# One edge pass for the first normalised layer: source-tile sums taken in the message pass, scatters all ahead of it

## The chip, the cores and the metric

The kernel runs on one core of a Trainium2 chip. The metric is the device time of one launch, in microseconds (us), lower is better. Engines: PE (TensorE), DVE (VectorE), ACT (ScalarE), POOL (GpSimd), SP (SyncE, which here only starts DMAs). PEld is PE's weight load, and a "q" behind an engine's name (SPq, DVEq) is its sequencer.

## What is computed

A graph of 3125 nodes and 53125 edges (sorted by destination) passes through four residual blocks, each followed by a layer norm. The lines that matter here are those of the second and the third:

```python
# block 1: messages over the edges
m_in = concatenate([h_node[src], h_node[dst], h_edge], axis=-1)
m = silu(m_in @ msg_W1 + msg_b1) @ msg_W2 + msg_b2
agg = segment_sum(m, dst)
h_new = silu(concatenate([h_node, agg]) @ upd_W1 + upd_b1) @ upd_W2 + upd_b2
# block 2: three layers with batch statistics over all edges
for l in range(3):
    x = concatenate([h[src], e], axis=1) @ W1[l].T + b1[l]
    x = (x - mean(x, axis=0)) * rsqrt(var(x, axis=0) + 1e-5) * gamma[l] + beta[l]
    m = relu(x) @ W2[l].T + b2[l]
    h = segment_sum(m, dst)
    if l < 2: h = relu(h); e = relu(e)
```

Block 0 is a GIN network and block 3 two SAGE layers; both work on a dense adjacency count and are not touched.

## The kernel before

Edges are cut into 104 groups of 512 (`NG`, `GE`; four chunks of 128 each, `GC`), and a loop over groups is written as 13 trips (`TRIPS`) of 8 (`UNROLL`). A pass over the edges works like this, for one group: POOL gathers the source rows with four indirect DMAs (L508); SP starts the load of the edge features (L522); PE multiplies these with the weights into PSUM (L1009 in block 1, L1050 in block 2; each f32 matmul of the code is two instructions of the trace); DVE adds the gathered rows (L1631, L1810) and in block 2 takes the maximum with a row (L1815); PE scatters the 512 messages into a window of 64 nodes by one-hot matrices that DVE makes (L532, L585); ACT copies the window out (L592), PE turns it (L599) and DVE adds it to the accumulator (L607). Each engine runs its own program in order and they meet only at semaphores; rings of eight edge slots and eight gather slots decouple them.

In the profiled execution the program has these stages, by its own times: to 549 us the setup and block 0, with the edges counted; 549 to 1095 the message pass of block 1; 1095 to 1141 its update; 1141 to 1690 pass A of layer 0; 1690 to 1878 pass B of layer 0; then for each of the layers 1 and 2 a table of 68 to 70 us and a merged loop of some 500 us, to 3016; to 3280 the SAGE layers.

**The edge rows by source tile.** For the statistics of layers 1 and 2 the kernel needs, for each of 25 tiles of 128 source nodes, the sum of relu(e) over the edges that leave each node, and the Gram matrix of relu(e). So POOL first copies all edge rows (128 features and the source's number, 132 floats) into `by_tile`, in the order of their source tile: 416 indirect scatters (L2285), in 208 pairs that SP loads. 376 of them stand ahead of block 1's gathers, 40 behind them. In pass A the rows are read back as units of 512 (L2497 loads a unit's first row into a register of SP, L2498 starts the DMA), 130 units, 10 per trip. Per unit ACT applies relu and a mask (L2153, four activations), DVE makes the one-hot (L1695), PE does eight instructions of 256 columns (L1061: one-hot and features side by side), and DVE adds the two halves of the result to the source sums `tA`, at a place that it loads into a register (L1700), and to `gram` (L1706, L1707).

**The two passes of layer 0.** Layers 1 and 2 have their statistics before the loop (from the sums) and run one merged pass. Layer 0 has not: pass A computes the pre-activations, adds them (L1768), writes them to `pre_dram` (96 DMAs of 512 KB from ACT's queue), squares them on ACT and sums the squares on DVE (L1758); then come the statistics, and pass B reads the pre-activations back, applies the maximum, and scatters. Its one-hots are made by POOL (L2388) and ACT.

**Block 1's targets.** Each group needs the 64 rows of its window of destination nodes. SP loads the window's start into a register (L2479) and starts two loads of these rows, one for each half of the partitions (L2481, `tabd`); ACT and DVE split them into three bf16 parts in the loop (L2091: three casts, L1618: two subtractions), and PE takes these with a one-hot of the destinations (L1013, L1016).

## Time and profile before

| | us |
|---|---|
| median of 3 runs | 3280.3 |
| lowest and highest | 3274.34, 3285.24 |
| the profiled execution's own time | 3281.03 |
| its span in the trace | 3279.8 |
| busy in the span: PE, DVE, POOL, ACT | 2644.0 (81%), 1990.8 (61%), 2157.4 (66%), 1272.0 (39%) |
| mean DMA rate | 174 GB/s |

The profiled execution lies 0.7 us above the median, so its spans can be used as they are. The share of a busy engine over the whole span says little here, since each stage has a limit of its own. The view of stretches gives, for each stage, the busy time of each engine and the clock that was granted to PE as a share of full speed; the timelines of one engine show the pace of one group; the rows of a source line show how often and for how long an instruction ran, and what ended the idle time before it.

### The profile page before, as it was taken

The numbers are of one execution on the slowest core, as the hardware profiler recorded it, in microseconds if no ns is written. First come the engines' busy times: TensorE is split into PE (matmuls) and PEld (weight loads), VectorE is DVE, ScalarE is ACT, GpSimd is POOL, SyncE is SP. The second block draws the span as 40 slices with busy tenths as digits, with TensorE's granted clock in tenths as the row PEclk, the third lists the DMA queues.
The fourth block names the chain that finished last, engine by engine and source line by source line (L and its number), as shares of the span: only waits on it lengthen the run. The fifth ranks groups of instructions, "written<-read, shape, count | busy, mean of one in ns | idle before, by whom it ended". The sixth has DMA issues, their size and how long they took to land. (4 is left out here: it accounts for less than half of the span.)

```text
span 3279.8 us, 59515 instructions
## 1 busy us (share of the span) xinstructions
PE 2644.0 (81%) x14026; PEld 1768.6 (54%) x14026; DVE 1990.8 (61%) x3581; ACT 1272.0 (39%) x3069; POOL 2157.4 (66%) x2211
## 2 busy tenths in 40 slices
PE   5689895776776878888889998777679867777998
PEld 2234443665665567777766656555446545555444
DVE  7998596544444567777779846555554655555111
ACT  4777514433333456666667622111112211112111
POOL 2777776777777677777758657777755777775000
PEclk7799998667667798999989999999989999988999
DMA  3344556655565489999959745555534555555000
GB/s 121 105 107 108 178 155 176 192 166 164 166 167 151 133 289 320 325 324 321 322 159 328 267 142 168 154 159 155 154 107 148 169 155 155 158 157 170 42 1 20
DMA packets 305074, 570.43 MB, mean 174 GB/s; under 512 B 54466, under 2 KB 140407, under 8 KB 303511
## 3 DMA queue, kind: packets, MB, share of 16 engines
q1 hardware_dynamic: 204582, 299.39, 29.8%
q0 software_dynamic: 86528, 219.09, 22.7%
q10 hardware_dynamic: 13824, 50.34, 3.8%
q8 instruction: 58, 0.95, 0.1%
q14 instruction: 82, 0.66, 0.1%
HBM read 465.21 MB, written 103.66 MB: 173 GB/s over the span
## 5 line engine op out<-in xcount | busy, mean ns | idle before, releaser
L508 POOL DMA_INDIRECT region<-tab,region x624 | 602.3, 965 | 285.4 <-issue 203.5
L1050 PE MATMUL psum<-w_all,region 128*128 128x256 f32 x2496 | 636.7, 400 | 0.7 <-ACT region L2161 0.7
L2285 POOL DMA_INDIRECT by_tile<-stage,place x416 | 407.1, 979 | 181.0 <-issue 126.3
L1050 PEld LDWEIGHTS psum<-w_all,region 128*128 128x128 f32 x2496 | 485.0, 201 | 66.1 <-issue 2.1
L592 ACT COPY region<-psum 128x256 f32<-128x256 f32 (+1 forms) x420 | 143.3, 341 | 850.5 <-PE psum L585 850.5
L585 PE MATMUL psum<-region 128*64 128x256 f32 (+1 forms) x1664 | 223.6, 393 | 192.2 <-DVE region L1815 122.1
L508 POOL DMA_INDIRECT tN<-tab,region x312 | 302.5, 970 | 95.1 <-issue 94.8
L508 POOL DMA_INDIRECT tA<-tab,region x312 | 298.3, 956 | 95.0 <-issue 94.4
L1061 PE MATMUL psum<-region 128*128 128x256 f32 x1040 | 281.0, 418 | 82.3 <-DVE region L1695 81.7
L599 PEld LDWEIGHTS psum<-fold,region 128*128 128x128 f32 x1470 | 215.9, 207 | 154.0 <-issue 153.8
L1061 PEld LDWEIGHTS psum<-region 128*128 128x128 f32 x1040 | 208.6, 208 | 136.6 <-issue 106.0
L599 PE MATMUL psum<-fold,region 128*128 128x64 f32 x1470 | 277.1, 309 | 0.0
L585 PEld LDWEIGHTS psum<-region 128*64 128x64 f32 x1664 | 115.1, 150 | 266.2 <-issue 178.3
L508 POOL DMA_INDIRECT region<-tabs,region x208 | 208.3, 1001 | 73.0 <-issue 70.2
L1810 DVE TENSOR_TENSOR psum<-region,psum 128x1024 f32<-128x1024 f32 x104 | 127.9, 1229 | 192.1 <-DMA region<-tab,region 175.6
L508 POOL DMA_INDIRECT tN<-tabs,region x208 | 201.9, 971 | 63.4 <-issue 60.3
L852 PE MATMUL psum<-region,acc 128*128 128x512 fp8e4 (+1 forms) x1050 | 205.5, 359 | 10.5 <-ACT acc L1958 7.5
L585 PE MATMUL psum<-tN,region 128*64 128x256 f32 (+1 forms) x1040 | 134.0, 385 | 98.9 <-DVE region L532 44.5
L2153 ACT ACTIVATE region<-region,part 128x128 f32<-128x128 f32 x524 | 166.2, 388 | 71.8 <-PE psum L1061 66.3
L1810 DVE TENSOR_TENSOR psum<-tA,psum 128x1024 f32<-128x1024 f32 x78 | 95.9, 1229 | 152.3 <-DMA tA<-tab,region 137.4
L1009 PE MATMUL psum<-w_all,region 128*128 128x128 f32 x832 | 176.5, 380 | 0.0
L2388 POOL TENSOR_TENSOR region<-node_no,dst_rel 128x256 f32<-128x256 f32 x104 | 134.7, 1295 | 55.7 <-ACT region L2195 42.2
(403 smaller groups left out, 4664.3 us busy)
## 6 DMA issues: line engine op xcount, KB each, us to landing
region<-e_t SPq DMA_DIRECT2D x416, 256.0 KB
region<-by_tile SPq DMA_DIRECT2D x131, 264.0 KB
stage<-e_rows SPq DMA_DIRECT2D x208, 132.0 KB
pre_dram<-region ACTq DMA_DIRECT2D x48, 512.0 KB, 6.0
pre_dram<-tN ACTq DMA_DIRECT2D x48, 512.0 KB, 5.6
region<-pre_dram SPq DMA_DIRECT2D x48, 512.0 KB
tN<-pre_dram SPq DMA_DIRECT2D x48, 512.0 KB, 5.1
tA<-dst_row SPq DMA_DIRECT2D x78, 256.0 KB
```

Of the source, the lines that this page charges most:

```text
L508: pool.indirect_dma_start(ring[j][:, c, at:at + width], None, table[:, :], bass.IndirectOffsetOnAxis(ap=idx[:, c:c + 1], axis=0)).then_inc ...
L585: mm = pe.matmul(acc_ps[at:at + WIN, j % 2, 0:halves * D], oh_ring[:, j % OH_SLOTS, c, :], ring[j][:, c, 0:halves * D], start=(c < 2), sto ...
L592: act.copy(win_ring[:, slot, 0:halves * D], acc_ps[:, slot, 0:halves * D]).then_inc(S["win_out"], 1)
L599: mm = pe.matmul(turned(slot)[:, h * WIN:(h + 1) * WIN], win_ring[:, slot, h * D:(h + 1) * D], fold[:, :], start=True, stop=True)
L852: mm = pe.matmul(psum[:, b, 0:hi - lo], parts[p][:, t, :], adj[:, t, lo:hi], start=(p == 0 and t == 0), stop=(p == 2 and t == N_TILES - 1))
L1009: pe.matmul(part, e_ring[:, j % E_SLOTS, edges], W("msg_e"), start=(c == 0), stop=False, skip_group_check=True)
L1050: mm = pe.matmul(banks[:, 2 * (j % 2) + c // 2, (c % 2) * 256:(c % 2) * 256 + 256], e_ring[:, j % E_SLOTS, c * D:(c + 1) * D], W(f"ee{l}") ...
L1061: mm = pe.matmul(unit_ps(m), u_both[:, m % 2, c, D:2 * D], u_both[:, m % 2, c, :], start=(c == 0), stop=(c == GC - 1))
L1810: dve.tensor_tensor(edge_ps(j), p, edge_ps(j), ALU.add).then_inc(S["pre"], 1)
L2153: r = act.activation(u_both[:, m % 2, c, D:2 * D], u_rows[:, m % U_ROWS, c, 0:D], ACT.Relu, scale=unit_mask[:, bass.ds(u * GC + c, 1)])
L2285: pool.indirect_dma_start(by_tile[:, :], bass.IndirectOffsetOnAxis(ap=place[:, 2 * q + c:2 * q + c + 1], axis=0), stage[:, k, c, :], None) ...
L2388: pool.tensor_tensor(off_ring[:, j % 2, :].rearrange("p (c n) -> p c n", c=GC), node_no[:, 0:WIN].unsqueeze(1).to_broadcast([D, GC, WIN]), ...
```

## The change

- `PUT_ENDS`: all 416 scatters stand ahead of block 1's gathers. The setup is reordered: the sources are loaded first, and their masks, counts and places are worked out ahead of the destinations' windows.
- Units become steps of two pieces of 256 rows, each with its own start in `by_tile` and its own place: 117 steps, 9 per trip (`UNITS_AT`: one per group, two at the last of eight). They run twice. Inside block 1's message pass they give the sums and the Gram matrix of the raw features, which layer 0's statistics now use; inside layer 0's pass those of the relu'd features, for layers 1 and 2.
- A step costs: on SP two register loads and two DMAs (L2367, L2368); on ACT four activations (L2055); on DVE two comparisons (L1646), two register loads (L1654) and two additions (L1662), the second behind a wait for the first; on PE eight instructions of 128 columns for the pieces and eight for the Gram matrix. The latter stays in a PSUM bank through the pass (bank 3, which block 1's single turned window leaves free, and later a bank of the scatter windows), so DVE's additions of it are gone.
- The rings: `U_ROWS` goes from 5 to 3, and two of the three slots are the buffers of the scatters (`stage`), so SP and DVE wait for the end of all scatters before the first step. `LAG` goes from 3 to 2, one turned window in PSUM instead of two, and layer 0 has one bank for the scatter window.
- Layer 0 is a merged pass like layers 1 and 2: the same loop, with the steps in it, no relu of the edge slots, one-hots on DVE. Pass A's squares and sums, `pre_dram` with its 96 writes and 96 reads, and pass B with POOL's one-hots are gone.
- The three bf16 parts of the targets are made once for all nodes, in the blocks that make the tables (eight more DMAs store them as `tgt_hi` and `tgt_low`); in block 1's loop SP loads parts (L2360, L2361) and the three casts and two subtractions are gone.

```diff
-LAG = 3
+LAG = 2
...
-PUT_ENDS = (0, 128, 188, PAIRS)
-
-
-UNITS_AT = [range(10 * j // UNROLL, 10 * (j + 1) // UNROLL) for j in range(UNROLL)]
-UNITS = 10 * TRIPS
-assert UNITS >= (EP + N_TILES * (GE - 1)) // GE
-TABLE = UNITS + 2
-U_ROWS = 5
...
+PUT_ENDS = (0, 128, PAIRS)
...
+PER_TRIP = UNROLL + 1
+UNITS_AT = [range(PER_TRIP * j // UNROLL, PER_TRIP * (j + 1) // UNROLL) for j in range(UNROLL)]
+UNITS = PER_TRIP * TRIPS
+PIECE = GE // 2
+PIECES = 2 * UNITS
+assert PIECES >= (EP + N_TILES * (PIECE - 1)) // PIECE
+TABLE = PIECES + 2
+U_ROWS = 3
...
+        u_rows = [stage[:, 2 * k:2 * k + 2, :, :].rearrange("p a b f -> p (a b) f") for k in range(2)] + [
+            row_spare.rearrange("p (c f) -> p c f", c=GC)]
+        node_sums = [raw_sums, xT, xT]
+
+        pieces_ps = st_ps[:, 0:2 * D]
+        message_gram, layer_gram = banks[:, 3, 0:D + 2], acc_ps[:, 1, 0:D + 2]
...
+            def source_units(i, j, gram_ps):
+                for m in UNITS_AT[j]:
+                    u = i * PER_TRIP + m
+                    lane, edge = u_lane[:, m % U_ROWS, :, :], u_rows[m % U_ROWS]
+                    pe.wait_ge(S["u_made"], T["u_made"] + u + 1)
+                    pe.nop(nofuse=True)
+                    pe.wait_ge(S["u_taken"], T["u_taken"] + u + 1)
+                    pe.nop(nofuse=True)
+                    pe.wait_ge(S["u_add"], T["u_add"] + 2 * u + 2)
+                    for c in range(GC):
+                        h = c // 2
+                        pe.matmul(pieces_ps[:, h * D:(h + 1) * D], lane[:, c, :], edge[:, c, 0:D], start=(c % 2 == 0), stop=(c % 2 == 1))
+                    for c in range(GC):
+                        mm = pe.matmul(gram_ps, edge[:, c, 0:D], edge[:, c, 0:D + 2], start=False, stop=(c == GC - 1),
+                                       skip_group_check=True)
+                    mm.then_inc(S["u_mm"], 1)
...
+                    source_units(i, j, message_gram)
...
+            def unit_prepare(u, i, m):
+                slot = m % U_ROWS
+                dve.wait_ge(S[f"from_dram{slot}"], T[f"from_dram{slot}"] + 32 * (PER_TRIP // U_ROWS * i + m // U_ROWS + 1))
+                dve.nop(nofuse=True)
+                dve.wait_ge(S["u_mm"], T["u_mm"] + u - 2)
+                for h in range(2):
+                    part = slice(2 * h, 2 * h + 2)
+                    made = dve.scalar_tensor_tensor(out=u_lane[:, slot, part, :], in0=node_no[:, :].unsqueeze(1).to_broadcast([D, 2, D]),
+                                                    scalar=unit_node[:, bass.ds(u * 2 + h, 1)],
+                                                    in1=u_rows[slot][:, part, D:D + 1].bitcast(I32).to_broadcast([D, 2, D]),
+                                                    op0=ALU.add, op1=ALU.is_equal)
+                made.then_inc(S["u_made"], 1)
+
+            def unit_places(u):
+
+                return [dve.value_load(unit_i[0:1, bass.ds(u * 2 + (TABLE - 2 + h), 1)], min_val=0, max_val=NP - D) for h in range(2)]
+
+            def unit_add(u, places, sums):
+
+                dve.wait_ge(S["u_mm"], T["u_mm"] + u)
+                for h, at in enumerate(places):
+                    dve.wait_ge(S["u_add"], T["u_add"] + 2 * u + h)
+                    to = sums[:, bass.ds(at, D)]
+                    dve.tensor_tensor(to, to, pieces_ps[:, h * D:(h + 1) * D], ALU.add).then_inc(S["u_add"], 1)
...
+            def merged_pass(l, bet):
+                dve.wait_ge(S["st_mm"], T["st_mm"] + 1)
+                dve.scalar_tensor_tensor(out=low_diag, in0=acc_ps[:, 0, 0:2 * D], scalar=2.0, in1=W(f"ee{l}"),
+                                         op0=ALU.mult, op1=ALU.mult).then_inc(S["stat_in"], 1)
+                dve.wait_ge(S["st_mm"], T["st_mm"] + 2)
+                v.did(dve.memset(a0, 0.0))
+                count_tables(T)
+                turned_shift(l, statistics(bet, merged_ps, a1, acc_ps[:, 1 if l else 0, 0:2 * D]))
+                if l == 0:
+                    units_clear(xT)
+                    unit_prepare(0, 0, 0)
                 with dve.Fori(0, TRIPS) as i:
                     for j in range(UNROLL):
                         g = i * UNROLL + j
-                        dve.wait_ge(S[f"rows_in{j}"], T[f"rows_in{j}"] + 16 * GC * (i + 1))
-                        dve.wait_ge(S["ve_mm"], T["ve_mm"] + g + 1)
-                        p = m_ring[j].rearrange("p c f -> p (c f)")
-                        dve.tensor_tensor(p, p, edge_ps(j), ALU.add).then_inc(S["pre"], 1)
-                        places = [unit_place(i * 10 + m) for m in UNITS_AT[j]]
-                        if j:
-                            add_squares(g - 1, j - 1)
-                        for m, at in zip(UNITS_AT[j], places):
-                            unit_prepare(i * 10 + m + 1, i, m + 1)
-                            unit_add(i * 10 + m, m, at)
-                    add_squares(g, j)
-                count_edges2(T, l)
-                dve.wait_ge(S["sq_add"], T["sq_add"])
-                dve.wait_ge(v.sem, v.did(dve.tensor_tensor(sq_acc[:, 0:4 * D], sq_acc[:, 0:4 * D], sq_acc[:, 4 * D:8 * D], ALU.add)))
-                dve.tensor_tensor(sq_acc[:, 0:2 * D], sq_acc[:, 0:2 * D], sq_acc[:, 2 * D:4 * D], ALU.add
-                                  ).then_inc(S["stat_in"], 1)
-                vrow_mm = statistics(bet, window_ps, sq_acc)
-
-                dve.wait_ge(S["pre"], T["pre"])
-                with dve.Fori(0, TRIPS) as i:
-                    for j in range(UNROLL):
-                        g = i * UNROLL + j
-                        p = m_ring[j]
-                        dve.wait_ge(S[f"from_dram{j}"], T[f"from_dram{j}"] + 16 * i)
-                        dve.tensor_tensor(p, p, low[:, :].unsqueeze(1).to_broadcast([D, GC, 2 * D]), ALU.max
-                                          ).then_inc(S["msg"], 1)
-                        w0 = dve_window_start(dve, g - LAG)
-                        dve_wide(dve, T, wide, g, sums2)
-                        dve_window(dve, T, g, w0, (j + LAG) % 2, 2)
-                finish(l, window_ps, vrow_mm)
-                count_sum2(T)
-
-            def merged_pass(l, bet):
-                dve.wait_ge(S["st_mm"], T["st_mm"] + 1)
-                dve.tensor_tensor(low_diag, acc_ps[:, 0, 0:2 * D], W(f"ee{l}"), ALU.mult).then_inc(S["stat_in"], 1)
-                dve.wait_ge(S["st_mm"], T["st_mm"] + 2)
-                v.did(dve.memset(a0, 0.0))
-                count_tables(T)
-                turned_shift(l, statistics(bet, merged_ps, a1))
-                with dve.Fori(0, TRIPS) as i:
-                    for j in range(UNROLL):
-                        g = i * UNROLL + j
+                        if l == 0:
+                            places = group_places(i, j)
...
+            def take_units(units, func):
+                for u, i, m in units:
+                    slot = m % U_ROWS
+                    act.wait_ge(S[f"from_dram{slot}"], T[f"from_dram{slot}"] + 32 * (PER_TRIP // U_ROWS * i + m // U_ROWS + 1))
+                    act.nop(nofuse=True)
+                    for c in range(GC):
+                        e = u_rows[slot][:, c, 0:D]
+                        r = act.activation(e, e, func, scale=unit_mask[:, bass.ds(u * GC + c, 1)])
+                    r.then_inc(S["u_taken"], 1)
...
-            put_rows(*PUT_ENDS[2:4])
...
-                for half in (slice(0, WIN), UPPER):
-                    sp.dma_start(tabd_ring[half, slot, :], tabd[bass.ds(w0, WIN), :]).then_inc(S[f"slot_in{slot}"], 16)
+                sp.dma_start(tgt_ring[0:WIN, slot, 0, :], tgt_hi[bass.ds(w0, WIN), :]).then_inc(S[f"slot_in{slot}"], 16)
+                sp.dma_start(tgt_ring[UPPER, slot, :, :].rearrange("p k f -> p (k f)"), tgt_low[bass.ds(w0, WIN), :]
+                             ).then_inc(S[f"slot_in{slot}"], 16)
+
+            def load_unit(u, m):
+                slot = m % U_ROWS
+                for h in range(2):
+                    row = sp.value_load(unit_i[0:1, bass.ds(u * 2 + h, 1)], min_val=0, max_val=EP - 1)
+                    sp.dma_start(u_rows[slot][:, 2 * h:2 * h + 2, :].rearrange("p c f -> p (c f)"),
+                                 by_tile[bass.ds(row, PIECE), :].rearrange("(p c) f -> p (c f)", c=2)
+                                 ).then_inc(S[f"from_dram{slot}"], 16)
+
+            def next_unit(u, m):
+                sp.wait_ge(S["u_mm"], T["u_mm"] + u - U_ROWS + 1)
+                sp.nop(nofuse=True)
+                load_unit(u, m)
+
+            def last_units():
+                for u in range((TRIPS - 1) * PER_TRIP + U_ROWS, UNITS + 1):
+                    next_unit(u, u % PER_TRIP)
 
             for j in range(UNROLL):
                 load1(j, j)
+            for k in range(STAGES):
+                sp.wait_ge(S[f"put{k}"], 32 * PAIRS // STAGES)
+            sp.wait_ge(S["idx_all"], 32)
+            sp.wait_ge(S["tile_tables"], 3)
+            for m in range(U_ROWS):
+                load_unit(m, m)
```

Three places show how the rows of an engine change. First **SP in block 1's loop**, before; the row above these is the group's load of the edge features. `w_i` is the table of window starts.

```order
L522 ISA [waits ve_mm]
L522 DMA region<-e_t 128x512
L2477 DMA tA<-dst_row 128x512 [waits ohT]
L2479 ISA
L2479 TENSOR_LOAD w_i
L2479 ISA x2
L2481 ISA
L2481 DMA region<-tabd 64x128 x2
```

After, from the load of the window's start (the two loads ahead of it are as before). `part` holds the table of the pieces' starts.

```order
L2359 TENSOR_LOAD w_i
L2359 ISA x2
L2360 ISA
L2360 DMA region<-tgt_hi 64x128
L2361 ISA
L2361 DMA region<-tgt_low 64x256
L2373 ISA
L2367 ISA [waits u_mm]
L2367 TENSOR_LOAD part
L2367 ISA x2
L2368 ISA
L2368 DMA stage<-by_tile 128x264
```

The last four rows stand there twice in each step. So a group has six DMAs and three register loads where it had four and one, and one group in eight has eight and five.

Second, **DVE in layer 0's loop**, before (pass A, one group).

```order
L1768 TENSOR_TENSOR region<-region,psum 128x1024 [waits ve_mm]
L1700 ISA
L1700 TENSOR_LOAD part2
L1700 ISA x2
L1757 REGISTER_ALU [waits sq]
L1758 TENSOR_TENSOR acc<-acc,psum 128x1024 [waits sq_add]
L1695 ISA [waits from_dram2,u_mm]
L1695 SCALAR_TENSOR_TENSOR region<-node_no,part2,region 128x4x128
L1704 REGISTER_ALU
L1706 ISA [waits u_add,u_mm]
L1706 TENSOR_TENSOR tA<-tA,psum 128x128
L1707 TENSOR_TENSOR region<-region,psum 128x128
```

After, the end of a group; ahead of it stand the two register loads of places, the addition of the gathered rows (L1773), the one-hot (L520) and the maximum (L1778).

```order
L595 ISA [waits sc_add,win_t]
L595 TENSOR_TENSOR acc<-acc,psum 128x2x64
L1658 REGISTER_ALU
L1660 REGISTER_ALU [waits u_mm]
L1662 ISA [waits u_add]
L1662 TENSOR_TENSOR region<-region,psum 128x128
L1660 REGISTER_ALU
L1662 ISA [waits u_add]
L1662 TENSOR_TENSOR region<-region,psum 128x128
L1646 ISA [waits from_dram2,u_mm]
L1646 SCALAR_TENSOR_TENSOR deg_lane<-node_no,part2,region 128x256
```

The addition of a step's sums now stands ahead of the next step's comparisons, and each of the two pieces has a row of its own. In a group with two steps the second step's addition waits for PE's work on the first.

Third, **PE in block 1's loop**, after: the turn of the window (L587), then the step, then the next group's edge product (L999). Before, L599 stood directly ahead of L1009.

```order
L573 MATMUL psum<-region 64x128 x3
L587 MATMUL psum<-fold,region 128x64 [waits win_out,sc_add]
L1030 MATMUL psum<-region,deg_lane 128x128 [waits u_made,u_taken,u_add]
L1030 MATMUL psum<-region,deg_lane 128x128 x3
L1032 MATMUL psum<-region 128x130 x4
L999 MATMUL psum<-w_all,region 128x128 [waits pre,slot_in4]
L999 MATMUL psum<-w_all,region 128x128 x3
```

Eight matmuls, sixteen instructions of the trace, are put into each group, behind waits for DVE's one-hots, ACT's mask and DVE's last addition.

## Rows read from the trace of the kernel before

**Rows 1.** Stretches: length, busy us of PE, PEld, DVE, ACT, POOL, clock, DMA

```profile
549.00:1095.00 546.00, 389.30 (x2710) 318.97 (x2710) 258.99 (x646) 198.44 (x569) 416.21 (x422) 0.69 0.59 165
...
1141.00:1690.00 549.00, 465.59 (x1915) 378.57 (x1916) 399.10 (x610) 332.51 (x840) 407.63 (x416) 0.92 0.90 307
1690.00:1878.00 188.00, 178.78 (x1303) 113.34 (x1303) 165.86 (x241) 132.77 (x324) 134.67 (x104) 0.96 0.78 274
...
1946.00:2448.00 502.00, 380.96 (x2076) 266.39 (x2075) 302.39 (x423) 93.35 (x205) 369.08 (x385) 0.95 0.53 153
```

**Rows 2.** L508 in block 1 (ns min/median/max, first and last start us)

```profile
L508 POOL DMA_INDIRECT region<-tabs,region x208: 940/944/4032, 550.4 to 1065.5; - x104
L508 POOL DMA_INDIRECT tN<-tabs,region x208: 940/944/1462, 573.9 to 1086.1; - x104
its engine sat idle before it (us, times) until:
  issue: 130.6, 397
```

**Rows 3.** L1631 in block 1: what ended DVE's idle time before it

```profile
  DMA tN<-tabs,region: 90.9, 46
  DMA region<-tabs,region: 72.8, 39
```

**Rows 4.** SP's queue in block 1: start us, us, instruction; one group and the next

```profile
576.92 0.34 SPq L522 DMA_DIRECT2D region<-e_t  x1
577.43 0.34 SPq L2477 DMA_DIRECT2D tA<-dst_row  x1
578.64 1.28 SPq L2481 DMA_DIRECT2D region<-tabd  x2
580.15 0.40 SPq L522 DMA_DIRECT2D region<-e_t  x1
...
583.26 0.40 SPq L522 DMA_DIRECT2D region<-e_t  x1
```

**Rows 5.** SP's queue at the start of pass A, five units without a wait

```profile
1144.62 4.77 SPq L2498 DMA_DIRECT2D region<-by_tile  x5
```

**Rows 6.** L2285, the scatters, ahead of block 1 and behind it

```profile
L2285 POOL DMA_INDIRECT by_tile<-stage,place x376: 953/958/1908, 53.3 to 539.6; - x188
...
L2285 POOL DMA_INDIRECT by_tile<-stage,place x40: 954/958/1171, 1087.4 to 1136.9; - x40
```

**Rows 7.** PE's timeline in block 1, about one group at full clock

```profile
809.44 0.66 PE L585 MATMUL psum<-region 128*64 128x128 f32 x8 [1.11 <-ACT region L592]
810.03 0.43 PE L599 MATMUL psum<-fold,region 128*128 128x64 f32 x2
810.30 1.11 PE L1009 MATMUL psum<-w_all,region 128*128 128x128 f32 x8
811.25 0.39 PE L1013 MATMUL psum<-region 128*128 128x128 bf16 x4
811.57 0.39 PE L1016 MATMUL psum<-region 64*128 64x128 bf16 x4
```

**Rows 8.** DVE's timeline in layer 1's loop, one group

```profile
2202.38 1.23 DVE L1810 TENSOR_TENSOR psum<-region,psum 128x1024 f32<-128x1024 f32 x1 [2.01 <-DMA region<-tab,region]
2203.51 0.42 DVE L532 TENSOR_TENSOR region<-node_no,dst_rel 128x256 f32<-128x256 f32 x1
2203.85 1.22 DVE L1815 TENSOR_TENSOR region<-psum,low 128x1024 f32<-128x1024 f32 x1
2204.98 0.28 DVE L607 TENSOR_TENSOR acc<-acc,psum 128x128 f32 x1
```

**Rows 9.** DVE's timeline in pass A, a group with two units

```profile
1504.33 1.22 DVE L1768 TENSOR_TENSOR region<-region,psum 128x1024 f32<-128x1024 f32 x1 [1.14 <-DMA region<-tab,region]
1505.91 1.22 DVE L1758 TENSOR_TENSOR acc<-acc,psum 128x1024 f32<-128x1024 f32 x1 [0.36 <-issue]
1507.04 0.75 DVE L1695 SCALAR_TENSOR_TENSOR region<-node_no,part,region 128x512 f32<-128x512 f32 x1
...
1511.94 0.29 DVE L1706 TENSOR_TENSOR tA<-tA,psum 128x128 f32 x1 [3.09 <-PE psum L1061]
```

**Rows 10.** PE's timeline in layer 1's loop, one group

```profile
2202.19 1.95 PE L1050 MATMUL psum<-w_all,region 128*128 128x256 f32 x8
2205.60 1.08 PE L585 MATMUL psum<-region 128*64 128x256 f32 x8 [1.46 <-DVE region L1815]
...
2207.11 1.08 PE L1050 MATMUL psum<-w_all,region 128*128 128x256 f32 x4
```

**Rows 11.** PE's timeline in pass A at the lower clock

```profile
1405.73 3.75 PE L1061 MATMUL psum<-region 128*128 128x256 f32 x8 [3.01 <-DVE region L1695]
```

**Rows 12.** L508 in layer 0 and in layer 1, L1810 in layer 1: first instructions of each

```profile
L508 POOL DMA_INDIRECT region<-tab,region x208: 942/946/3980, 1148.1 to 1660.5; - x104
...
L508 POOL DMA_INDIRECT region<-tab,region x208: 942/946/1192, 1907.1 to 2416.4; - x104
...
L1810 DVE TENSOR_TENSOR psum<-region,psum x52: 1228/1230/1230, 1946.1 to 2420.2; 128x1024 f32<-128x1024 f32 x52
...
L1810 DVE TENSOR_TENSOR psum<-tN,psum x13: 1228/1229/1230, 1970.8 to 2440.5; 128x1024 f32<-128x1024 f32 x13
```

737 lines of the change are left out of this document (278 added, 459 removed).

## The prediction

> **What bounds the kernel now.** I read the view of stretches first, to see which stages the change touches and how full each engine is there [rows 1]. Block 1's pass lasts 546 us, layer 0's two passes 549 and 188; PE is the fullest engine in them, with 389 of 546, 466 of 549 and 179 of 188 us, but a full engine is not yet the limit, so for each stage I looked for the engine whose instructions follow each other without a cause to wait.
>
> In block 1 that is POOL. Its 416 gathers start from 550.4 to 1086.1 us, and nearly all its idle time is "issue" [rows 2]: the next gather is simply not started faster. That is 535.7/415 = 1.29 us per gather, 5.16 per group, 41.3 per trip of eight groups. DVE agrees: the idle time before its addition ends with a gather's landing [rows 3]. The same holds in layer 1, where the first and the last addition of 104 stand at 1946.1 and 2440.5 [rows 12]: 494.4/103 = 4.80 per group, and a timeline shows DVE waiting 2.01 us for a gather [rows 8].
>
> In pass A of layer 0 gathers start from 1148.1 on; the DMA engines are busy to 0.90 with 307 GB/s, because of the 96 writes, and PE is nearly full. Pass B is bound by PE (179 of 188).
>
> The last queue to look at is SP's, since the change adds to it in every group. In block 1, where nothing holds it up yet, one group's loads start 3.23 and 3.11 us after the former's [rows 4]. So SP is busy for 3.11 of 5.16 us, for four DMAs and one register load. In pass A five units of one register load and one DMA each lie in 4.77 us, with four distances and a last DMA of 0.33 us: (4.77 - 0.33)/4 = 1.11 us per piece [rows 5].
>
> **Setup and scatters.** 40 more scatters stand ahead of block 1. They took 1087.4 to 1136.9 us, 49.5/39 = 1.27 us each [rows 6], so 51 us; there they lay beside the update, on no path, so nothing comes back for them. The first one now follows masks and counts without the windows' setup ahead of it. It started at 53.3; I estimate about 38, by the work that no longer stands ahead of it, with both ends 53 and 35. The 376 scatters ended at 540.5; now 416 end at 540.5 + 51 - 15 = about 577 (590 if nothing is gained at the start). The counting and block 0 run beside them and gain some 2 us from the earlier start: -2. Their tables were there at about 549, and the parts of the targets add a few short steps and eight DMAs to them; SP's first loads then start at some 557.
>
> **Block 1.** SP per group: as before 3.11 (the same number of DMAs, and of partitions in each). Per step two pieces of 1.11, and some 0.28 for the wait and the registers of the loop: 2.5. A trip is 8 x 3.11 + 9 x 2.5 + 0.3 for the loop = 24.9 + 22.5 + 0.3 = 47.7 us, 5.96 per group, against 41.3 of POOL. That is the new limit, if the rows of the idle queue hold in the loop. The others: DVE is busy 259/104 = 2.49 per group, and a step adds two comparisons (half of 0.75 each [rows 9]), two additions of 0.28 and two register loads that cost at most 1.58 (1504.33 to 1505.91, a group with two of them [rows 9]): 2.9 x 9/8 = 3.3, in all 5.8 with the subtractions that in fact go, and some 5.1 without them. PE at full clock is 2.52 per group, from 809.44 to 811.96 [rows 7], plus a step of 16 instructions of 128 columns, whose distance is 0.95/8 = 0.119 (810.30 to 811.25), with the Gram matrix's two extra columns 1.95: 1.95 x 9/8 = 2.2, in all 4.7. ACT is busy 198/104 = 1.9 per group [rows 1], loses three casts and gains four activations. None reaches 5.96.
>
> The stage then runs so: first loads of eight groups from 557 to 582, scatters at their end about 577, three steps of 2.5 to 590. Twelve trips of 47.7 us are 572: the last loads stand at 1162. SP is five groups ahead of the step that it serves, so six groups of about 5 us and a last landing follow, 37 us: 1199, where it was 1095. **+104.** If the two loads of targets, 1.28 us together, took what two of the first kind would (0.51 between starts and 0.34 for the last, 0.85 [rows 4]), a trip would be 3.4 us shorter: 12 x 3.4 = 41, +63. At 2.6 per step it is +115.
>
> **Layer 0.** Before, from 1141 to 1878: 737 us. After, its loop is layer 1's with the steps in it. From the start of the stage to the first addition: layer 1's gathers begin at 1907.1 and its first addition is at 1946.1, 39 us, and here gathers began 7 us after the stage's start [rows 12]: 46, and 3 more to clear the sums and prepare the first step. Then the pace. PE at full clock: scatter and turn 2205.60 to 2207.11, 1.51; the edge product eight instructions at a distance of (1.95 - 1.08)/4 = 0.22, 1.78 [rows 10]; a step 1.95; 0.1 for the semaphores: 5.34. DVE: 2202.38 to 2205.26, 2.88 [rows 8]; two additions with a wait between 0.66, two comparisons 0.8, two register loads, of whose 1.58 about 0.74 lies beside the comparisons, 0.85: 5.19. So PE sets 5.34, with DVE close to it, and both above the gathers' 4.80. In a group with two steps the second one's addition waits for PE's work on the first, as today (3.09 us at 1511.94 [rows 9]); with the second step's own 1.46 of DVE work that is 4.5 per trip. A trip is 8 x 5.34 + 4.5 + 0.3 = 47.5; 13 are 618; with 5 at the end 46 + 3 + 618 + 5 = 672. **-65.** At 5.5 us per group, all waits counted, it would be -111; at 6.4 it is -17. The passes' DMAs cost nothing now: 96 writes and reads of 512 KB go, and the rate falls to some 180 GB/s, so no stage is near 307.
>
> The shorter `LAG` I cost at nothing: in layer 1 PE has finished the turn at 2207.11, 5 us before DVE wants it one group on [rows 8, 10]; if that cover went, it would be at most 1.5 per group in two layers. Layers 1, 2 and the SAGE layers stay within 3 us.
>
> Sum: 3281.0 - 2 + 104 - 65 = 3318, 1.1% above the median of 3280.3 (the profiled run lies 0.7 us above it).
>
> **A rule against it.** The rows show SP's queue at 3.11 us per group and 1.11 per piece without a wait, as long as or longer than a group of other engines' work. The Trainium skill ("DMA: Bandwidth & Descriptors", section "Issuing engines are not separate DMA queues") says that the sequencer's time to start a DMA is usually small beside the DMA itself. By that rule SP would not set the pace and the first rival below would hold; by the rows, it does. The trace does not agree with the rule for these small loads.
>
> **The rivals.**
> 1. *SP's issue hides.* POOL keeps block 1's pace, and only the later start counts: gathers start at 578 instead of 550.4, +28. Then 3281 - 2 + 28 - 65 = 3242, faster by 1.2%. It decides at the price of a piece: a trip of SP is 25.2 + 18 p, equal to 41.3 at p = 0.90 us. Against it stand 1.11 of [rows 5]; for it, that some of this may run under the waits of the loop, and that I have not seen four DMAs and two pieces in a row.
> 2. *The steps in layer 0 hide beneath the gathers*, at 4.80 per group: 46 + 499 + 6 = 551, -186, with block 1 as forecast 3281 - 2 + 104 - 186 = 3197. Against it: DVE's and PE's sums are both above 5.1, before any wait. For it: PE's and DVE's rows show pieces that overlap a little. With rival 1 too it is 3121.
> 3. *PE does not keep its clock*, the case on the far side of the forecast. In block 1 the granted clock was 0.69, with PE busy 71% [rows 1], and in pass A a unit's eight instructions of 256 columns took 3.75 us after a wait of 3 us [rows 11], where full clock gives 1.78. If the new waits between steps leave the mean clock of layer 0 near 0.85 instead of 0.95, 5.34 becomes 5.9 and with the two-step group 6.5: 46 + 3 + 676 + 5 = 730, -7, and the time is 3281 - 2 + 104 - 7 = 3376. In block 1 the clock would have to stay below 4.7/5.96 = 0.79 to matter; at 0.69 the group is 6.8 and the time rises by another 80, but an engine that is so full was granted 0.92 to 0.96 in the other stages [rows 1].
>
> **How the numbers follow.** The forecast case has 0.50, with its own range 3280 to 3365 from the bounds of both stages; rival 1 has 0.15, rival 2 0.12, both together 0.04, rival 3 0.15, and 0.04 is left. A measurement tells 0.3%, 10 us, from no change. Faster by more: rivals 1 and 2, both, and a bit of the rest, 0.33. Within 0.3%: 0.08 of the forecast case and 0.02 of the rest, 0.10. Slower: the remaining 0.57. The range leaves out the case of both rivals and the ends of rival 3: 3195 to 3380.
>
> **What would show it.** SP's queue in block 1 with DMAs end to end and no gap, and a trip of 47 to 48 us; DVE's addition there waiting for edge loads by way of PE, or POOL waiting for PE, and no longer for gathers; the last scatter at 575 to 590. In layer 0 additions 5.9 us apart on average, with one long wait for PE in every eighth group. Wrong would be a block 1 at 41 us per trip (the price of a piece), or a layer 0 above 6.3 or at 4.8 per group (the clock, or the overlap), or layers 1 and 2 slower than 4.8 (`LAG`).

## The result and the profile after

The changed kernel takes 3469.0 us (median of 4 runs, 3466.95 to 3470.6) against 3281.8 for the kernel before: 1.0572 times its time, 95% interval 1.0557 to 1.0588. The forecast was 3318 with a range of 3195 to 3380. The direction was right; 151 us were missing.

The profiled execution took 3470.55 us, with a span of 3469.3. Its stretches, as in [rows 1] (length, busy us of PE, PEld, DVE, ACT and POOL, granted clock, DMA share, GB/s): block 1's pass and layer 0.

```profile
597.00:1279.00 682.00, 527.04 (x4568) 473.85 (x4568) 374.54 (x906) 246.26 (x717) 407.43 (x416) 0.88 0.62 177
...
1327.00:2068.00 741.00, 639.05 (x4135) 504.54 (x4134) 481.56 (x929) 195.41 (x589) 399.93 (x416) 0.94 0.53 157
```

Block 1 lasts 682 us instead of 546 and starts at 597 instead of 549; layer 0 lasts 741 instead of 737. So the merging of the two passes brought nothing. The gathers, answering to [rows 2] and [rows 12] (ns min/median/max, first and last start us; block 1 first, then the three layers together):

```profile
L496 POOL DMA_INDIRECT region<-tabs,region x208: 938/944/1431, 597.4 to 1219.3; - x104
L496 POOL DMA_INDIRECT tN<-tabs,region x208: 938/944/3426, 617.9 to 1240.2; - x104
its engine sat idle before it (us, times) until:
  issue: 139.0, 362
  PE psum L573: 113.3, 54
...
L496 POOL DMA_INDIRECT region<-tab,region x624: 940/946/1201, 1334.9 to 3174.0; - x156
```

POOL now waits 113 us for PE to free the slots: it has ceased to set the pace. Layer 0's gathers begin at 1334.9 instead of 1148.1, +187, where the sum had +102. Layer 1's begin at 2098.7 instead of 1907.1, so layer 0 takes 763.8 us instead of 759.0, +5, where the sum had -65. Layers 1 and 2 keep their pace: 37.9 and 37.8 us per trip of additions, 38.2 and 38.0 before.

The additions of gathered rows, block 1 (L1596, answers to L1631) and layer 0 (L1773), the first groups of rows of each:

```profile
L1596 DVE TENSOR_TENSOR region<-region,psum x52: 686/687/689, 631.1 to 1255.1; 128x512 f32<-128x512 f32 x52
...
L1773 DVE TENSOR_TENSOR psum<-region,psum x52: 1228/1229/1230, 1380.2 to 2030.4; 128x1024 f32<-128x1024 f32 x52
```

In block 1 the first stands at 631.1 and 12 trips later comes one at 1243.0: 51.0 us per trip, forecast 47.7. In layer 0 the trips are 52.8 us in the same way (1380.2 to 2014.0 for 12), forecast 47.5. Three things are to be explained, then: the late start, and two paces.

**The start.** SP's queue before block 1 (start us, us, instruction):

```profile
560.60 13.30 SPq L2284 DMA_DIRECT2D stage<-e_rows  x6
574.61 0.38 SPq L2340 DMA_DIRECT2D tabs<-tN  x1
...
596.60 1.25 SPq L2332 DMA_DIRECT2D tgt_low<-acc  x1
599.71 0.34 SPq L510 DMA_DIRECT2D region<-e_t  x1
```

and DVE's timeline there:

```profile
540.90 0.06 DVE L1575 MEMSET small<- 128x1 f32 x1
604.49 0.69 DVE L1581 TENSOR_TENSOR region<-tA,win_node 128x512 bf16<-128x512 int32 x1 [63.53 <-DMA region<-tgt_low]
```

DVE has finished the tables at 541 us. Their stores stand on SP behind the loads of the scatters' last pairs, which go on until 573.9 because each waits for a scatter; then come 17 DMAs, and the first edge load at 599.7. The scatters themselves ran from 37.4 to 580.5, as forecast (38 and 577).

**The pace of block 1.** SP's queue in the middle of the loop, one group from 903.63 to 909.36 and the next to 914.92:

```profile
903.63 0.33 SPq L510 DMA_DIRECT2D region<-e_t  x1
904.12 0.33 SPq L2357 DMA_DIRECT2D tA<-dst_row  x1
905.42 0.50 SPq L2360 DMA_DIRECT2D region<-tgt_hi  x1
906.11 0.48 SPq L2361 DMA_DIRECT2D region<-tgt_low  x1
907.61 1.51 SPq L2368 DMA_DIRECT2D region<-by_tile  x2
909.36 0.33 SPq L510 DMA_DIRECT2D region<-e_t  x1
...
914.92 0.33 SPq L510 DMA_DIRECT2D region<-e_t  x1
```

There is no gap: 5.6 to 5.7 us for a group with one step, as the sum had it (3.11 + 2.5). But once per trip SP stands still for 2.9 to 3.7 us, and that stop is not SP's own: it is gone in the runs where DVE has no pause.

**The pauses.** DVE's sequencer at the end of a trip, in layer 0 and in block 1 (L1765 and L1689 are the loops' own lines; the same columns):

```profile
L1765 DVEq COMPARE_BRANCH  x1: 56/56/56, 1532.5 to 1532.5; - x1
L1765 DVEq FUSED_REGOPS  x1: 98/98/98, 1535.7 to 1535.7; - x1
...
L1689 DVEq COMPARE_BRANCH  x1: 56/56/56, 831.2 to 831.2; - x1
L1689 DVEq FUSED_REGOPS  x1: 74/74/74, 834.6 to 834.6; - x1
```

The jump back is executed at 1532.5 and the first instruction at the loop's top at 1535.7. No wait stands between them. This is so at each of the 11 jumps back in block 1 and the 12 in layer 0, with 2.9 to 4.0 us each; in the kernel before every such jump took 0.3 us, and in this kernel's layers 1 and 2 it still does. What it does to the engines, on DVE and then on PE:

```profile
1524.65 1.23 DVE L1773 TENSOR_TENSOR psum<-tN,psum 128x1024 f32<-128x1024 f32 x1 [2.64 <-issue]
...
1531.49 0.71 DVE L1662 TENSOR_TENSOR region<-region,psum 128x128 f32 x2 [2.52 <-PE psum L1032]
1532.26 0.88 DVE L1646 SCALAR_TENSOR_TENSOR deg_lane<-node_no,part,stage 128x256 f32<-128x256 f32 x2
1537.38 1.23 DVE L1773 TENSOR_TENSOR psum<-region,psum 128x1024 f32<-128x1024 f32 x1 [4.23 <-issue]
```

```profile
1540.56 1.98 PE L573 MATMUL psum<-region 128*64 128x256 f32 x8 [4.53 <-DVE region L1778]
```

The idle time of 4.23 us before DVE's addition at 1537.38 is the pause and the register loads behind it. The 2.64 us before the addition at 1524.65 are no pause: this group has two steps, so four places are loaded ahead of it, one behind the other:

```profile
L1654 DVEq TENSOR_LOAD <-part x4: 300/308/322, 1521.4 to 1523.9; - x4
```

PE idles 4.53 us and then works at half clock (1.2 of 2.4 GHz): L573 takes 1.98 us instead of the 1.08 of [rows 10]. The stretches around it say it in one number each, the clock in the third column from the end:

```profile
1492.20:1540.00 47.80, 41.69 (x291) 33.77 (x289) 32.59 (x63) 12.81 (x40) 29.73 (x32) 1.00 0.63 184
1540.00:1546.80 6.80, 6.24 (x28) 5.12 (x29) 4.52 (x10) 1.55 (x5) 2.83 (x3) 0.50 0.13 40
```

Part 3 of the page shows a sign of the cause. The queue of instructions carried 82 packets before and 199 after, 117 more for 23 pauses, five for each:

```profile
q14 instruction: 199, 1.63, 0.2%
```

### The profile page after: what moved, and what is told of

The parts are those of the page before. It is cut to its first block and busy times, and to the rows that moved or that the text cites. A ratio compares the mean times of both kernels' runs of the same rounds, so it can differ in the third digit from the quotient of the medians.

```text
span 3469.3 us, 68487 instructions
## 1 busy us (share of the span) xinstructions
PE 2777.0 (80%) x16815; PEld 1937.4 (56%) x16815; DVE 2029.7 (59%) x3935; ACT 1055.0 (30%) x2653; POOL 2011.7 (58%) x2107
## 3 DMA queue, kind: packets, MB, share of 16 engines
q1 hardware_dynamic: 246390, 278.22, 27.7%
## 5 line engine op out<-in xcount | busy, mean ns | idle before, releaser
L496 POOL DMA_INDIRECT tA<-tab,region x468 | 448.6, 959 | 149.3 <-issue 144.4
L573 PE MATMUL psum<-region 128*64 128x256 f32 (+1 forms) x1664 | 224.9, 394 | 202.8 <-DVE region L1778 174.9
L1773 DVE TENSOR_TENSOR psum<-region,psum 128x1024 f32<-128x1024 f32 x156 | 191.7, 1229 | 275.0 <-DMA region<-tab,region 174.4
L2055 ACT ACTIVATE stage<-stage,part 128x128 f32<-128x128 f32 x632 | 201.9, 390 | 350.5 <-DMA stage<-by_tile 345.7
L587 PEld LDWEIGHTS psum<-fold,region 128*128 128x128 f32 x1470 | 211.8, 204 | 156.4 <-issue 156.4
L587 PE MATMUL psum<-fold,region 128*128 128x64 f32 x1470 | 271.9, 305 | 6.2 <-issue 5.7
L573 PEld LDWEIGHTS psum<-region 128*64 128x64 f32 x1664 | 111.8, 147 | 290.3 <-issue 238.8
L1773 DVE TENSOR_TENSOR psum<-tA,psum 128x1024 f32<-128x1024 f32 x117 | 143.8, 1229 | 177.0 <-DMA tA<-tab,region 138.1
L1662 DVE TENSOR_TENSOR region<-region,psum 128x128 f32 x472 | 134.9, 286 | 119.8 <-PE psum L1032 83.9
L520 DVE TENSOR_TENSOR region<-node_no,dst_rel 128x256 f32<-128x256 f32 x416 | 175.5, 422 | 48.8 <-issue 48.2
L1030 PE MATMUL psum<-stage,deg_lane 128*128 128x128 f32 x1248 | 203.5, 314 | 0.0
L573 PE MATMUL psum<-tA,region 128*64 128x256 f32 x936 | 129.7, 397 | 92.0 <-DVE tA L1778 91.7
L1778 DVE TENSOR_TENSOR region<-psum,low 128x1024 f32<-128x1024 f32 x156 | 189.8, 1217 | 0.0
L1032 PE MATMUL psum<-stage 128*128 128x130 f32 x1248 | 186.9, 299 | 0.0
```

Of the source, the lines that this page charges most:

```text
L496: pool.indirect_dma_start(ring[j][:, c, at:at + width], None, table[:, :], bass.IndirectOffsetOnAxis(ap=idx[:, c:c + 1], axis=0)).then_inc ...
L520: dve.tensor_tensor(oh_ring[:, j % OH_SLOTS, :, :], node_no[:, 0:WIN].unsqueeze(1).to_broadcast([D, GC, WIN]), dst_rel[:, bass.ds(g * GC, ...
L573: mm = pe.matmul(acc_ps[at:at + WIN, j % slots, 0:halves * D], oh_ring[:, j % OH_SLOTS, c, :], ring[j][:, c, 0:halves * D], start=(c < 2), ...
L587: mm = pe.matmul(turned[:, h * WIN:(h + 1) * WIN], win_ring[:, slot, h * D:(h + 1) * D], fold[:, :], start=True, stop=True)
L1030: pe.matmul(pieces_ps[:, h * D:(h + 1) * D], lane[:, c, :], edge[:, c, 0:D], start=(c % 2 == 0), stop=(c % 2 == 1))
L1032: mm = pe.matmul(gram_ps, edge[:, c, 0:D], edge[:, c, 0:D + 2], start=False, stop=(c == GC - 1), skip_group_check=True)
```

## The experiments

Two groups of four runs (e5 to e8 and those that begin with c) fell on two chips on which the gathers came late: the kernel before takes 4228 and 4275 us there, and a trip of block 1 in the changed kernel 69.3 us instead of 51.0 (c_after). Each run is compared with the kernel before on its own chip. The experiments' four kernels on the first of these chips were run again on a chip like the first (d); c_after is the changed kernel itself.

**Shorter code for DVE.** The branches for wide windows, which this graph never takes, are left out of DVE's two loops:

```diff
-                with dve.If(wide > 0):
-                    dve.wait_ge(S[f"rows_x{j}"], 16 * GC * (i + 1))
...
-                dve_wide(dve, T, wide, g, sums1)
...
-                        dve_wide(dve, T, wide, g, sums2)
+                        if l:
+                            dve_wide(dve, T, wide, g, sums2)
```

> The changed kernel, with the code for wide windows left out of DVE's two loops that have steps in them (block 1 and layer 0). That code stands behind a branch that this graph never takes, so DVE's work and order stay as they are, and only the loops' bodies get shorter: 398 instructions to about 250 in block 1, 380 to about 285 in layer 0. Theory 'code': in the changed kernel DVE stands still for 2.9 to 4.0 us behind each jump back to the top of these two loops (11 and 12 times), and in the kernel before for 0.3 us, because the body is now too long to be kept. Then the pauses go in the loop whose body is short enough: block 1's trip falls from 51.3 to 47.5 us, where SP's queue of 47.0 sets it, and layer 0's from 52.8 to 47 to 49; in all 3469 - 45 - 55 = about 3370. Should 285 still be too long, only block 1 gains: about 3424. Rival 'ring': the end of a trip is late because two steps stand in one group and only three slots are there; the pause lies beside waits for the ring. Then the trips stay at 51 and 52 us and the time at 3460 or more.

Measured: 3467.4 us, 1.0546 (1.0501 to 1.0592). Nothing changed, and the pauses stayed, with 2.8 to 4.0 us. By itself this speaks against the length of the code. But the bodies have 294 and 284 instructions, so block 1's is not the 250 that I had expected, and the next run decides. (These counts, like the others in the expectations, leave out the waits for a semaphore that stand alone; the trace has 323 and 300 records of DVE per trip, with them.)

**Dead code in the kernel before.**

```diff
                         dve_wide(dve, T, wide, g, sums2)
+                        with dve.If(wide > 0):
+                            for _ in range(24 if l == 1 else 6):
+                                dve.memset(small[:, 0:1], 0.0)
```

> The kernel before, with code that is never executed put into DVE's loop of layer 1 (24 instructions per group, body from 204 to about 420) and of layer 2 (6 per group, to about 276). Theory 'code': in layer 1 DVE pauses 3 to 4 us behind the jump back in each of 12 trips, in layer 2 either so too or, if 276 still fits, 0.3 us. DVE has about 2 us of slack per group there, and eight slots of gathered rows, so the time rises by less than 10 us. If length is not the cause, both loops keep 0.3 us.

Measured: 3282.3 us in a single run, within 7 us of the kernel before (3288.6 on its chip). Layer 1's loop (412 instructions) pauses for 3.3 to 4.5 us in every trip, layer 2's (270) for 0.3 us. One jump of each, from DVE's sequencer:

```profile
L1804 DVEq COMPARE_BRANCH  x1: 56/56/56, 2118.5 to 2118.5; - x1
L1804 DVEq FUSED_REGOPS  x1: 74/74/74, 2122.2 to 2122.2; - x1
...
L1804 DVEq COMPARE_BRANCH  x1: 56/56/56, 2607.5 to 2607.5; - x1
L1804 DVEq FUSED_REGOPS  x1: 74/74/74, 2607.8 to 2607.8; - x1
```

```profile
q14 instruction: 143, 1.17, 0.1%
```

Code that is never executed makes the pause, so it comes with the length of a loop's body; by these counts the limit lies between 270 (none) and 284 instructions. Twelve pauses brought 61 more packets, again five each. And a pause costs nothing where DVE has slack: layer 1, where DVE waits 2 us per group for gathers [rows 8], took 38.1 us per trip, and 38.2 before.

**The stores between the pairs.** SP's stores of the tables are put between the last three batches of four pairs:

```diff
-            load_pairs(PUT_ENDS[1] + SPILLS * STAGES, PUT_ENDS[2])
-            count_rows(T)
+            load_pairs(PUT_ENDS[1] + SPILLS * STAGES, PAIRS - 3 * STAGES)
...
                 stored, before = tiles.stop, (n, tiles)
+                k = (1, 3, 5, 6).index(n)
+                if k < 3:
+                    load_pairs(PAIRS - (3 - k) * STAGES, PAIRS - (2 - k) * STAGES)
             store_parts(*before)
+            count_rows(T)
```

> The changed kernel, with the stores of the tables on SP's queue put between the last 12 pairs of the edge rows' loads, three batches ahead of the end, instead of behind them. In the changed kernel DVE has made the tables by 541 us, but the first store stands at 574.6, behind the last load of a pair, and 25 us of stores and the first edge load at 599.7 follow. Theory 'queue order': the first edge load comes 15 to 20 us earlier, at 580 to 585, and all that follows too: 3450 to 3454. Rival: the scatters, which end at 581, or their buffers set the start of the steps, and SP's batches hold up the scatters in turn, so that less than 5 us come back.

Measured: 3459.6 us, 1.0523 (1.0483 to 1.0563), about 9 less, between the two expectations. The first edge load stands at 588.8 instead of 599.7, the gathers start at 590.5 instead of 597.4 and the first addition stands at 620.5 instead of 631.1, but the scatters now end at 590 instead of 581: part of the gain is given back, since the stores hold up the pairs. So the queue order is shown as a cause of the late start, worth 9 to 11 us of the 41. That the other 30 are the 17 DMAs' own 23 us on this queue, and the late end of the pairs, is argued: no run started them from another queue.

**ACT starts two loads.** As in the first experiment, and in block 1's loop ACT issues the loads of the edge features and destinations for the group eight ahead (SP keeps the targets and the steps, behind one wait for PE):

```diff
                     silu1(i, j)
+                    g = (i + 1) * UNROLL + j
+                    sp_load_e(act, T, g, j)
+                    act.wait_ge(S["ohT"], T["ohT"] + g - (E_SLOTS - 1))
+                    act.nop(nofuse=True)
+                    act.dma_start(dst_ring[j % E_SLOTS], dst_row[bass.ds(g, 1), :].partition_broadcast(D)
+                                  .rearrange("p a f -> p (a f)")).then_inc(S[f"slot_in{j % E_SLOTS}"], 16)
```

> As the first of these kernels, and in block 1's loop ACT instead of SP starts the loads of the edge features and of the destinations for the group eight ahead (about 1.05 us per group less on SP). Theory 'issue': with the pause gone, block 1's pace is SP's queue of 47.0 us per trip; this takes it to 38.6, and the next limit is POOL's 41.3 or DVE with its two-step group: a trip of 42 to 45, so 30 to 60 us less than the first kernel, some 3320 to 3340. Rival: SP is full only because nothing faster asks for it, and the trip is set by DVE, PE and the ring: within 10 us of the first kernel.

Measured: 3413.7 us, 1.0383 (1.0344 to 1.0423), 54 less than without it. Block 1's trip falls from 50.8 to 46.3 us. That is SP's issue, shown even with the pauses in place, in the range of the expected gain; the trip is a little above the 42 to 45 that it named, as the pauses are still there. Layer 0's trip stays at 52.8.

**Straight code.** DVE's two loops are written out in trips (block 1's is shown, layer 0's is done likewise):

```diff
-            with dve.Fori(0, TRIPS - 1) as i:
+            for i in range(TRIPS - 1):
```

> The changed kernel, with DVE's loops over trips in block 1 and layer 0 written out as straight code: the same instructions in the same order, no jump back. The run with shorter bodies kept its pauses with bodies of 294 and 284 instructions, and of the kernel before with dead code the loop of 412 got them and the loop of 270 did not; so theory 'code' stands with its limit between 270 and 284. It expects here no pauses at the trips' ends, block 1's trip at 47 to 48 us (SP's queue) instead of 51.0, layer 0's at 46 to 48 instead of 52.8, where PE's idle time and its fall to the lower clock go too: 3469 - 40 - 65 = about 3365. If straight code has to be waited for as well, the pauses are spread over the loop and the time stays above 3450. Rival 'ring': the pauses hide waits for the ring and for the second step, and less than 20 us come back.

> The changed kernel as it is, as the measure for the three kernels beside it on the same chip: 3469 us, if this chip is like the first one. The four kernels before ran on a chip where the kernel before took 4228 us instead of 3280, with gathers that came late in every stage, so their times say nothing in us of the first chip; they are run again here.

> DVE's two loops written out as straight code. Theory 'code': no pause at the trips' ends, block 1's trip at 47 to 48 us, layer 0's at 46 to 48: 3469 - 40 - 65 = about 3365. Rival 'ring': less than 20 us come back, since the pauses only cover waits for the ring and for the second step.

> DVE's two loops as straight code, once more, for a chip like the first. Theory 'code': block 1's trip 47 to 48 us (SP's queue), layer 0's 46 to 48, no pause at the trips' ends: about 3365. On the slow chip it was 87 us less than the changed kernel. Rival 'ring': above 3440.

On the late chips it took 1.0115 (1.0046 to 1.0184) and 1.0102 (1.0063 to 1.014) of the kernel before, where the changed kernel takes 1.0306 (1.025 to 1.0361): 87 us less. On a chip like the first it took 3338.8 us, 1.0166 (1.0146 to 1.0186), 130 less than the changed kernel, and more than any theory had said. No pause is left, the instruction queue has 136 packets, and SP's queue in block 1 runs without a stop, a trip of 48.1 us. Layer 0's loop, the stretch from 1352 to 1930 us with the columns of the first view:

```profile
1352.00:1930.00 578.00, 558.20 (x3905) 450.87 (x3904) 448.28 (x872) 183.38 (x563) 370.01 (x384) 1.00 0.64 186
```

PE is busy for 558 of 578 us at full clock, and a trip is 45.2 us. But straight code does a second thing: addresses are constants, so DVE's group shrank from 5.2 to 4.7 us. Two more runs bear on this.

**Every second jump.** The loops are cut into loops of two trips each, with the same body (again block 1's is shown):

```diff
-            with dve.Fori(0, TRIPS - 1) as i:
+            for trip in range(0, TRIPS - 1, 2):
+              with dve.Fori(trip, trip + 2) as i:
```

> The changed kernel, with DVE's loops of 12 and 13 trips in block 1 and layer 0 cut into loops of two trips each, one behind the other: the same body with addresses from registers, but one jump back in two trips. Theory 'pause': every second trip has the pause of 3 to 4 us and the other has not; a layer 0 trip with it takes 52 to 53 us and one without 46 to 48, and half of the pauses' price comes back: 3469 - 45 = about 3420 (between 3405 and 3440). Theory 'register work': the addresses cost the time, trips differ by less than 2 us, and the kernel stays above 3455.

Measured: 3443.6 us, 1.0474 (1.0443 to 1.0505), 25 less. Trips with a pause and trips without one alternate. In block 1 they take 50.7 to 52.4 and 46.3 to 48.2 us: the pause costs 3.9 us there (51.5 and 47.6 in the mean), and without it the trip is the one of SP's queue. In layer 0 they take 51.5 to 54.9 and 49.7 to 51.0 (52.9 and 50.5 in the mean): a difference of some 2 us. But PE's fall to the lower clock comes behind the pause, in the trip that is counted as one without. The same 6.8 us behind a pause and behind a jump without one, the clock in the third column from the end:

```profile
1522.40:1529.20 6.80, 6.27 (x28) 5.15 (x29) 4.49 (x10) 1.55 (x5) 2.84 (x3) 0.50 0.17 33
1572.40:1579.20 6.80, 5.56 (x40) 4.43 (x42) 5.56 (x13) 2.52 (x9) 2.92 (x4) 1.00 0.39 111
```

So the stretch must run from the eighth group's addition of one trip to that of the next, with the jump and all that follows it inside. These stretches take 48.4 to 48.8 us without a pause (1560.34 to 1609.11, at full clock throughout) and 53.8 to 57.1 with one (1609.11 to 1662.96). Layer 0 without pauses would thus take some 48.6 us per trip, 4 less than the 52.8 of the changed kernel, and the last 3.4 us down to the 45.2 of straight code are something else. The time is just above the range that theory 'pause' gave, and its 46 to 48 us for a trip without one is missed by a little. Theory 'register work' alone would have left the trips equal. One jump with a pause, and one from a loop's end to the next loop, 0.2 us:

```profile
L1767 DVEq COMPARE_BRANCH  x1: 56/56/56, 1411.3 to 1411.3; - x1
L1767 DVEq FUSED_REGOPS  x1: 104/104/104, 1414.8 to 1414.8; - x1
...
L1767 DVEq COMPARE_BRANCH  x1: 50/50/50, 1465.5 to 1465.5; - x1
...
L1767 DVEq FUSED_REGOPS  x1: 98/98/98, 1465.7 to 1465.7; - x1
```

**Loops kept, bodies below the limit.** The first experiment, and one place per step instead of two on DVE (both pieces are added at the first one's place, so the source sums, and with them the statistics, are not the reference's):

```diff
-                return [dve.value_load(unit_i[0:1, bass.ds(u * 2 + (TABLE - 2 + h), 1)], min_val=0, max_val=NP - D) for h in range(2)]
+                return [dve.value_load(unit_i[0:1, bass.ds(u * 2 + (TABLE - 2), 1)], min_val=0, max_val=NP - D)] * 2
```

> As e1_dve_code, and the place of a step's second piece is left out: DVE loads one place per step instead of two and adds both pieces' sums there, so the source sums are not those of the reference. The bodies fall from 294 and 284 instructions to about 249 and 239. Theory 'pause' with a limit between 270 and 284: no pause at either jump back (0.3 us), block 1's trip 47 to 48 us (SP's queue), layer 0's 45 to 47: 3355 to 3385. If the pause were that of loops with steps in them and not of the length, both loops would keep it.

Measured: 3341.5 us, 1.0163 (1.0133 to 1.0194), the time of straight code. Bodies of 249 and 239 instructions have no pause, with steps and loops in place. One jump of block 1:

```profile
L1683 DVEq COMPARE_BRANCH  x1: 56/56/56, 915.6 to 915.6; - x1
L1683 DVEq FUSED_REGOPS  x1: 74/74/74, 915.9 to 915.9; - x1
```

With the waits that stand alone the trace has 278 and 255 records of DVE per trip, against 323 and 300 in the first experiment, whose loops pause; so, with every instruction counted, the limit lies between 278 and 300. Block 1's loop stands at the same place of DVE's program in both kernels, since nothing ahead of it differs, so there it is the length and not the place. Whether the place moves the limit between 278 and 300 no run shows.

Trips are 48.0 and 45.3 us. DVE in layer 0, a whole group and the start of the next, and then one group of the first experiment, whose body differs in the second place alone:

```profile
1529.00 1.23 DVE L1767 TENSOR_TENSOR psum<-region,psum 128x1024 f32<-128x1024 f32 x1
...
1533.32 1.23 DVE L1767 TENSOR_TENSOR psum<-region,psum 128x1024 f32<-128x1024 f32 x1
...
1536.60 0.61 DVE L1656 TENSOR_TENSOR region<-region,psum 128x128 f32 x2 [0.40 <-PE psum L1032]
```

```profile
1543.33 1.23 DVE L1767 TENSOR_TENSOR psum<-region,psum 128x1024 f32<-128x1024 f32 x1 [0.81 <-PE psum L1066]
...
1548.58 1.23 DVE L1767 TENSOR_TENSOR psum<-region,psum 128x1024 f32<-128x1024 f32 x1 [0.79 <-issue]
```

DVE needs 4.32 us for a group with one register load of a place, and 5.25 with two (5.35 in the changed kernel from 1537.38 to 1542.73, 5.25 from 1549.63 to 1554.88), while PE needs 5.17. The branches for wide windows are gone in the first experiment and present in the changed kernel, with the same 5.25: they cost DVE nothing here. That is the second cause in layer 0: with two loads DVE has nothing in hand against PE, least in the group with four loads. With 0.5 to 0.9 us per group in hand DVE runs ahead, PE is hardly ever idle, and the trip is PE's own work.

**The ninth step.** With straight code, group 4 has two steps, one ahead of the scatter and one behind, instead of two in a row in group 7:

```diff
-UNITS_AT = [range(PER_TRIP * j // UNROLL, PER_TRIP * (j + 1) // UNROLL) for j in range(UNROLL)]
+UNITS_AT = [(0,), (1,), (2,), (3,), (4, 5), (6,), (7,), (8,)]
...
+                    source_units(i, STEPS_EARLY[j], message_gram)
                     scatter1(i, j)
-                    source_units(i, j, message_gram)
+                    source_units(i, STEPS_LATE[j], message_gram)
```

> As e5_unrolled, and the ninth step of a trip stands elsewhere: group 4 has two steps, one of them ahead of the group's maximum on DVE and of its scatter on PE, one behind, instead of two in a row at the end of group 7. Theory 'two steps': in layer 0 two steps in a row make DVE wait 2.5 us for PE and PE 1.0 us for DVE, and let the gathers and slots run late behind them; a trip without that is 8 x 5.18 + about 2.6 = 44 us, 2 to 4 less than in e5_unrolled: 25 to 50 us. Rival: the step's own work on DVE and PE is the price, wherever it stands: within 10 us of e5_unrolled.

> As c_unrolled, with the ninth step in the middle of a group instead of behind another. Theory 'two steps': layer 0's trip 2 to 4 us shorter than in c_unrolled, 25 to 50 us in all. Rival: its own work is its price, wherever it stands: within 10 us of c_unrolled.

> The ninth step in the middle of a group as well. Theory 'two steps': layer 0's trip at about 44 us, 25 to 50 us less than d_unrolled (29 on the slow chip). Block 1 stays at SP's 47.

Measured on a chip like the first: 3323.9 us, 1.0120 (1.01 to 1.0141), 15 less than d_unrolled; layer 0's trip goes from 45.2 to 44.3 us. On the late chips 38 and 29 us. So two steps in a row cost 1 us per trip when DVE is fast, less than I had put, and more where gathers come late.

**All edits.** Straight code, ACT's loads and the stores between the pairs, without and with the ninth step in the middle:

> As e5_unrolled, and ACT starts the loads of edge features and destinations in block 1's loop, and the stores of the tables stand between the last loads of pairs (9 us when alone). Theory 'issue': with the pauses gone SP's 47.0 us per trip are the bound of block 1, and this lifts it: trips of 42 to 44 us, so 35 to 55 us less than e5_unrolled for the loads and 9 for the stores, about 3310. If DVE, PE and the ring set the trip with the pauses gone, it stays within 15 us of e5_unrolled.

> As d_unrolled, with ACT's loads in block 1 and the stores between the pairs. Theory 'issue': block 1's trip 42 to 44 us instead of 47, 35 to 55 us less than d_unrolled, and 9 for the stores: about 3310. If DVE, PE and the ring set block 1's trip, it stays within 15 us of d_unrolled.

> All four edits together: DVE's loops written out, ACT's loads in block 1, the stores between the pairs, the ninth step in the middle. If the terms add up, e6_all_three less what e7_mid_step gains on e5_unrolled: about 3270 to 3285, the time of the kernel before. Below 3270 would mean that block 1 gains from the step's place too.

> All four edits: straight code, ACT's loads in block 1, stores between the pairs, the ninth step in the middle. If the terms add up (3469 - 105 for the pauses, - 40 for the issue, - 9, - 35) it is at 3280, no different from the kernel before; on the slow chip it was 1.1% faster than that.

> All four edits. By the sum of the terms 3265 to 3285, 1.1% below the kernel before as on the slow chip, or no different from it.

Measured: 3238.8 us, 0.9861 (0.9842 to 0.9881), and 3228.3 us, 0.9829 (0.9812 to 0.9845); on the late chips 0.9929 (0.986 to 0.9999) for the first, 0.9889 (0.9861 to 0.9918) and 0.9894 (0.9855 to 0.9934) for the second. The first is 100 us below d_unrolled, where I had expected 44 to 64: 85 us are block 1's 12 trips, and its first addition comes 15 us earlier. Its gathers in block 1:

```profile
L497 POOL DMA_INDIRECT region<-tabs,region x208: 940/945/3427, 583.5 to 1108.6; - x104
L497 POOL DMA_INDIRECT tN<-tabs,region x208: 940/946/1482, 606.7 to 1129.6; - x104
its engine sat idle before it (us, times) until:
  issue: 124.6, 409
  PE psum L574: 2.1, 7
```

Block 1's trip is 41.0 us, POOL's own pace as in [rows 2], with all the steps inside: 7 us less than d_unrolled in each trip. So with the pauses gone SP's issue was the whole bound, and the steps' work on the other engines costs nothing there. The last version takes 1.7% less than the kernel before and 7% less than the changed kernel.

## Why the prediction was wrong

**Right.** The scatters (37.4 to 580.5 us). SP's queue as block 1's bound: forecast 47.7 per trip, 48.0 wherever the pauses are gone, with no gap, and 41.0 when two loads leave the queue. So rival 1 is refuted; the Trainium skill's rule ("DMA: Bandwidth & Descriptors", section "Issuing engines are not separate DMA queues"), that starting a DMA is usually small beside the DMA, did not keep the queue from setting the pace: six to eight small loads of a group take 5.6 us and more to start here, and no other engine needs as long. The formula of rival 1, 25.2 + 18 p, leaves out the 0.28 per step that the sum has: with it, it is 27.7 + 18 p, which equals 41.3 at p = 0.76, so the rival was further off than it said. PE's group of 5.34 in layer 0 was 5.17. `LAG` costs nothing: layers 1 and 2 have 37.9 and 37.8 us per trip of additions, 38.2 and 38.0 before. Layer 0 has 45 us from its first gather to its first addition, 53 from its start (forecast 46 and 3). Rival 2 held in no run: the shortest trip of layer 0 is 44.3 us, PE's own work, and not the gathers' 38.4.

**Wrong, the start: 41 us.** The step "Their tables were there at about 549, and ... SP's first loads then start at some 557" failed. The tables were there at 541. But the edit moved 20 pairs of loads on SP ahead of their stores, and I had followed the 40 scatters only on POOL, the engine that executes them. The kernel before shows the same queue: there the stores began as soon as the pairs ended. A moved step must be followed on each queue that it issues on, as SP's here; the first loads came at 599.7, and block 1's first addition 41 us later than the sum had the steps ready. The order of SP's instructions would have shown it.

**Wrong, block 1's trips: 40 us.** 51.0 us instead of 47.7, in 12 trips, by the pauses at DVE's jump back: 48.1 without them. The step that failed is "+ 0.3 for the loop": the sum let every engine pass the loop's end without a stop, and DVE's stop of 2.9 to 4.0 us there holds up SP too. No row of the kernel before showed one, since no body of DVE's was longer than some 250 instructions; the change takes two of them to 398 and 380 (all these without the waits that stand alone). I counted busy time and issue time for each added instruction and none for the length of the code.

**Wrong, layer 0: 70 us.** The sum had 47.5 us per trip and the trace 52.8. Two steps of it failed.

- "8 x 5.34 + 4.5 + 0.3": the 0.3 for the loop. Some 4 us of the difference are the pause with PE's fall to the lower clock behind it, as f1_pairs shows (48.6 without them): 50 us in 12 trips.
- "with the second step's own 1.46 of DVE work that is 4.5 per trip": the other 1.1 us lie here, 14 us in all, since the groups with one step are as forecast (5.4 on average in f1_pairs). The term left out the second step's own two register loads, which stand ahead of the group's addition (the 2.64 us of "issue" at 1524.65). The two last groups take 6.67 and 9.7 us in f1_pairs, 6.0 more than two groups of 5.2.

The rest of the 70 is the start, 4 us more than 46 and 3. That the groups with one step came out near the forecast's 5.34 is in part luck: the step "So PE sets 5.34, with DVE close to it" put PE's group 0.17 too high and named the wrong engine, since DVE with its two register loads needs 5.25. In f2_short and d_unrolled, where DVE has 0.5 to 0.9 us in hand, the trip falls to 45.2 and is PE's, with 3.8 for the second step (45.2 - 8 x 5.17).

**Rival 3** had a like size (3376) by another way. The clock did fall, to half for 3 to 7 us once per trip, but behind a pause: the mean of layer 0 is 0.94, not 0.85, and in d_unrolled with the same PE work it is 1.00 through 578 us. Without the pauses and DVE's register loads the forecast would have been 21 us off (3339 against 3318), with the start 41 and block 1's end 9 too late and layer 0 27 better than summed.

**What stays open.** The pause's cause is shown to be the body's length on DVE, with the limit between 278 and 300 instructions, every one counted. Whether the limit depends on where the loop stands in the program is not shown. For the other engines no run looked for it; PE's loop in block 1 has 448 records per trip, and no such gap behind its jumps. No run has DVE's two loads per step in a short loop without a pause, so the 48.6 us for that case are put together from stretches of f1_pairs. How far the other register work of DVE counts is open too: in straight code, where addresses are constants and two loads are left, its group is 4.7 us.

## What to carry to other kernels

Count the instructions of a loop's body when a change adds to it, those of branches never taken too, and look at the time between a loop's jump back and its first instruction: it is a gap that no list of waits names ("issue"). Sum the issue of each queue per trip as one sums an engine's work, and follow a moved step on all queues that it issues on. Count the register loads that stand ahead of a group's first instruction, above all where a group has two steps: they run one behind the other. And where two engines that wait for each other need nearly the same time per group, a little less work on one (0.9 us per group of DVE here) takes waits off the other.

## What the runs showed of the hardware

With every instruction counted, as the trace records them, DVE loops of 255 and 278 instructions jump back in 0.3 us (f2_short) and loops of 300 and 323 in 2.8 to 4.0 (e1_dve_code). The same is so by the shorter count, without the waits that stand alone, for loops that hold code that is never executed: 0.3 us at 270, 2.8 to 4.5 at 380, 398 and 412. Each pause brings some five more packets on the instruction queue. The pause comes whether the extra instructions are executed or not, and the same work as straight code has none. Behind the pause of 3 to 4 us PE, which idled 4.5 us, ran at half clock for 3 to 7 us. On DVE one register load less per group took the group from 5.25 to 4.32 us (e1_dve_code, f2_short); the load itself shows 0.31 us, and one load follows the next at some 0.8 us (four from 1521.4 to 1523.9). Branches for wide windows that were never taken cost DVE nothing in layer 0.
